# Attention and a mixture of experts on one core: newly searched orders for all five engines, and GpSimd steps that also wait for a named step

## What is computed

```python
x = x + attn(layernorm(x))      # causal; 3 query and key channels a head, 8 value channels a head
x = x + moe(layernorm(x))

# attn: scores[t,s] = scale * q3[t].k3[s] + (q3[t].dir) * (k3[s].dir); softmax over s <= t; out @ wo
# moe, for each of the 4096 tokens:
shared = gelu(xf @ Wfc_s + bfc_s) @ Wproj_s + bproj_s                 # 128 -> 512 -> 128
topk_p, topk_i = top_k(softmax(xf @ Wr), 2)                           # 8 experts, the best two
routed = sum over the two of gate * (gelu(xf @ Wfc[e] + bfc[e]) @ Wproj[e] + bproj[e])
```

## Time and profile before

| | us |
|---|---|
| median of 3 timed runs | 649.78 (647.6 to 656.1) |
| span of the profiled execution, first to last instruction | 693.1 |

### The profile page before, as it was taken

One profiled execution on the slowest core, in us unless ns is written; L12 is line 12 of the kernel. 1 busy time (PEld: TensorE's weight loads), 2 busy tenths in 40 slices (PEclk: granted clock), 3 DMA queues, 4 the chain that ended last, 5 costly groups with the idle time before them and its releaser, 6 DMA issues.

```text
span 693.1 us, 15803 instructions
## 1 busy us (share of the span) xinstructions
PE 577.4 (83%) x5284; PEld 433.5 (63%) x5318; DVE 444.3 (64%) x1179; ACT 423.6 (61%) x711; POOL 324.1 (47%) x434
## 2 busy tenths in 40 slices
PE   2678898999899799898897899999897787478686
PEld 2455464665465466565485778787776575377686
DVE  7799977699995966789844534555431245264386
ACT  4355776375666686396594599989998153134231
POOL 6817256475854657486445011122513576431440
PEclk9899998999999999999999899999999799599899
DMA  6182630063733010011526476857767287277661
GB/s 168 32 296 87 193 122 5 27 183 92 204 122 95 13 29 20 16 32 50 208 63 205 146 223 200 256 177 240 240 204 232 82 259 232 72 210 268 195 194 52
DMA packets 62429, 99.48 MB, mean 144 GB/s; under 512 B 9020, under 2 KB 47840, under 8 KB 61920
## 3 DMA queue, kind: packets, MB, share of 16 engines
q1 hardware_dynamic: 58512, 90.62, 43.1%
q0 software_dynamic: 3840, 7.87, 3.6%
HBM read 83.37 MB, written 31.80 MB: 166 GB/s over the span
## 4 chain that ended last, share of the span: by engine, by line
PE 38%; DVE 25%; ACT 16%; issue 9%; another core or an unknown queue 6%; POOL 3%; DMA 2%; SPq 0%; POOLq 0%; DVEq 0%; ACTq 0%
DVE negmax L1063 11%; PE banks L1425 7%; PE banks L1504 6%; PE banks L1512 5%; ACT hblk L961 5%; PE banks L1335 4%; ACT probs L923 4%; PE banks L1384 4%; ACT L961 3%; PE banks L1487 2%; PE banks L1386 2%; DVE probs L1208 2%; ACT L923 2%; PE banks L1482 2%
## 5 line engine op out<-in xcount | busy, mean ns | idle before, releaser
L1063 DVE TENSOR_REDUCE negmax<-banks 128x2 f32<-128x1024 f32 (+3 forms) x192 | 192.2, 1038 | 40.1 <-PE banks L1386 32.1
L923 ACT ACTIVATE probs<-banks 128x1024 f32<-128x1024 f32 x160 | 156.0, 1025 | 31.8 <-PE banks L1406 19.8
L792 POOL TENSOR_SCALAR_AFFINE_SELECT probs<-probs 128x512 f32<-128x512 f32 x128 | 79.6, 640 | 183.4 <-ACT probs L923 182.7
L961 ACT ACTIVATE hblk<-banks,wcur 128x128 f32<-128x128 f32 x340 | 95.3, 376 | 99.2 <-PE banks L1504 53.5
L1504 PE MATMUL banks<-xblkT,wcur 128*128 128x128 f32 x680 | 99.7, 291 | 25.2 <-ACT hblk L961 10.9
L1384 PE MATMUL banks<-kpad,qst 128*128 128x384 bf16 (+3 forms) x478 | 107.2, 296 | 15.6 <-DVE negmax L1063 9.1
L1504 PEld LDWEIGHTS banks<-xblkT,wcur 128*128 128x128 f32 x680 | 88.8, 202 | 32.1 <-ACT hblk L961 13.4
L1512 PE MATMUL banks<-wcur,hblk 128*128 128x128 f32 x680 | 93.2, 281 | 10.6 <-ACT hblk L961 4.2
L1386 PE MATMUL banks<-future,identb 128*128 128x128 bf16 x512 | 96.4, 220 | 5.3 <-ACT probs L923 1.9
L1512 PEld LDWEIGHTS banks<-wcur,hblk 128*128 128x128 f32 x680 | 83.9, 194 | 17.0 <-issue 6.2
L830 POOL DMA_INDIRECT got<-ys,from_row x56 | 55.1, 984 | 68.3 <-issue 30.2
(11 more groups left out here) (157 smaller groups left out, 862.0 us busy)
## 6 DMA issues: line engine op xcount, KB each, us to landing
wcur<-wtab SPq DMA_DIRECT2D x85, 578.0 KB
xs<-in_L_attn_x SPq DMA_DIRECT2D x8, 1188.0 KB, 8.7
xblk<-xs SPq DMA_DIRECT2D x85, 64.0 KB
ys<-yblk SPq DMA_DIRECT2D x34, 128.0 KB
kpad<-kst SPq DMA_DIRECT2D x64, 64.0 KB, 3.0
xs<-in_L_attn_x SPq DMA_DIRECT2D x8, 505.0 KB
acc<-in_L_attn_x SPq DMA_DIRECT2D x8, 256.0 KB, 5.1
wtab<-in_L_ffn_Wfc SPq DMA_DIRECT2D x2, 1024.0 KB
```

What stands on the lines that cost most here:

```text
L792: pool.affine_select(out=v, in_=v, compare_op=ALU.is_ge, fill=0.0, base=0, pattern=[[0, R], [1, P]], channel_multiplier=-1).then_inc(maske ...
L923: nc.scalar.activation(probs[:, g % 2, heads[0]:heads[-1] + 1, at:at + P * sum(EUNITS[unit])], src, ACT.Exp).then_inc(exp_done, 1)
L961: ins = nc.scalar.activation(hblk[:, k % 3, q, :], one(PLACE["HB", g, s])[:, P * q:P * q + P], ACT.Gelu_apprx_tanh, bias=wcur[:, k % NW, 2 ...
L1063: dve.tensor_reduce(negmax[:, g, tiles - 1, heads[0]:heads[-1] + 1], unit_view(PLACE["M", b, n], tiles), AX.X, ALU.max, negate=True).then_ ...
```

## The change

No step is added to any list or taken from it: the five lists hold the same steps (781 TensorE, 393 ScalarE, 492 VectorE, 234 GpSimd, 228 SyncE) in another order. 689, 301, 437, 199 and 206 of the places hold another step than before. Three things can be read off the new lists.

- The ScalarE list changes between exponential and gelu 36 times, before 60 times. Of the 24 that are gone 22 lie between `GB.0.0` and `GB.1.0`, two around `LX.4.0`.
- TensorE steps that need a single bank were in banks 4 to 7 only; now 156 of them are in banks 0 to 3, 66 of these ahead of `XT.0.0`.
- GpSimd waits, ahead of 18 `SC` or `GA` steps, for one more semaphore (`PACE`).

```diff
+PACE = {
+    ('SC', 5, 1): ('MX', 7, 19),
+    ('GA', 1, 2): ('YB', 1, 5),
+    ('GA', 2, 3): ('HB', 1, 12),
+    ('SC', 7, 3): ('HB', 1, 13),
+    ('SC', 7, 1): ('HB', 1, 15),
+    ('SC', 7, 0): ('YB', 1, 16),
+    ('GA', 3, 2): ('HB', 2, 0),
+    ('GA', 4, 1): ('HB', 2, 1),
...
+    ('GA', 5, 2): ('SB', 2, 8),
+    ('GA', 6, 0): ('HB', 2, 11),
+    ('GA', 6, 1): ('SB', 2, 10),
+    ('GA', 6, 3): ('SB', 2, 11),
+}
...
+            def hold_apart(kind, b, i):
+
+                if (kind, b, i) in PACE:
+                    step, at, n = PACE[kind, b, i]
+                    if step == "HB":
+                        pool.wait_ge(hblk_ready, nth("HB", at, n))
...
+                    elif step == "SB":
+                        pool.wait_ge(sums_ready, nth("SB", at, n))
...
                 elif kind == "SC":
+                    hold_apart(kind, b, n)
                     send_rows(b, n)
                 elif kind == "GA":
+                    hold_apart(kind, b, n)
                     get_rows(b, n)
```

A stretch of the ScalarE list, before and after:

```diff
-    GB.0.28 EX.7.0 HE.6.0 EX.7.1 GB.0.29 GB.0.30 EX.7.4 GB.0.31 GB.0.32 EX.7.2 GB.0.33 X2.6.0 GB.0.34 EX.7.3
-    GB.0.35 LX.6.0 EX.7.5 EX.7.6 OE.7.0 GS.6.3 GB.0.36 GB.0.37 EX.7.7 GB.0.38 GB.0.39 EX.7.8 GB.0.40 GB.0.41
...
+    OE.6.2 GB.0.25 GB.0.26 GB.0.27 GB.0.28 EX.7.1 EX.7.0 EX.7.4 GB.0.29 HE.6.0 GB.0.30 GB.0.31 GB.0.32 GB.0.33
+    EX.7.2 GB.0.34 X2.6.0 EX.7.3 LX.6.0 EX.7.5 GB.0.36 GS.6.3 GB.0.35 GB.0.37 OE.7.0 EX.7.6 EX.7.9 EX.7.7 EX.7.8
```

More of the change, by code:

```diff
@@ L72 @@
[L72 to L76, removed]
@@ new lines @@
+    TP.1.1@7 E.1.11@4 M.2.6@0 Y.0.2@6 E.1.10@42 TP.1.2@7 RK.0.0@1 Y.0.3@6 TK.3.0@7 M.2.7@2 M.2.8@4 TM.2.0@6
+    TQ.3.0@0 PV.1.3@7 M.2.9@4 T1.4.0@6 TP.1.3@7 M.2.13@2 M.2.10@0 TO.1.0@7 E.2.0@24 PJ.1.0@7 TQ.3.1@1 E.2.2@4
+    TM.2.1@6 M.3.5@0 M.3.11@7 M.2.16@2 E.2.5@4 M.2.23@6 TK.3.1@7 M.2.12@0 E.2.1@24 QKV.4.0@7 M.2.14@0 M.2.18@4
+    T2.1.0@6 M.2.22@2 M.2.19@0 RL.1.0@6 H.1.2@5 H.1.3@7 QKV.4.1@6 M.2.20@2 H.1.1@4 M.2.15@0 H.1.0@7 E.2.3@42
+    PV.2.0@6 Y.1.0@7 E.2.4@20 Y.1.1@7 M.2.21@4 Y.1.2@7 TK.4.1@3 M.3.2@0 TM.2.2@6 M.3.1@4 TK.4.0@2 TP.2.0@6
@@ new lines @@
+    TK.5.1@5 T2.3.0@4 M.5.0@2 M.4.21@0 M.5.2@6 H.3.0@4 E.4.8@2 H.3.2@5 RL.3.0@1 TM.4.3@0 PV.4.1@3 H.3.3@2
+    H.3.1@5 E.4.10@60 M.5.10@2 Y.3.0@5 RK.3.0@4 Y.3.1@5 M.5.4@2 E.4.11@0 QKV.6.1@4 M.5.7@6 E.4.9@2 Y.3.2@5
+    E.4.7@6 Y.3.3@5 M.5.3@2 M.5.17@4 M.5.6@6 TP.4.1@5 M.5.12@0 PV.4.3@3 M.5.8@4 PV.4.2@2 TM.5.0@3 M.5.9@0
+    M.5.13@4 E.5.0@62 QKV.6.0@1 TP.4.2@0 E.5.1@42 TM.5.1@7 TP.4.3@6 M.5.15@2 M.5.16@0 TO.4.0@6 T1.7.0@7 M.5.18@4
+    E.5.5@2 PJ.4.0@6 E.5.2@0 M.5.23@5 E.5.4@62 M.5.14@0 M.5.22@2 TK.6.0@5 E.5.3@60 QKV.7.1@4 M.5.19@2 TQ.6.0@7
@@ new lines @@
+    E.6.6@40 M.7.18@6 Y.5.0@2 XT.0.8@3 Y.5.1@2 YB.0.12@3 E.6.9@64 E.6.11@0 YB.0.13@3 HB.0.14@7 HB.0.15@6
+    HB.0.17@3 XT.0.9@5 HB.0.16@4 M.7.19@0 YB.0.14@7 XT.0.10@5 YB.0.15@7 YB.0.16@6 E.6.10@40 Y.5.2@2 HB.0.18@7
+    YB.0.17@6 HB.0.19@3 XT.0.11@6 Y.5.3@2 M.7.22@0 HB.0.20@5 M.7.23@7 HB.0.21@4 YB.0.18@6 TP.6.1@7 YB.0.19@6
+    E.6.8@0 E.6.7@42 PV.6.3@7 HB.0.22@6 YB.0.20@1 XT.0.13@0 YB.0.21@1 M.7.0@2 HB.0.23@7 XT.0.12@1 M.7.20@4
+    M.7.3@2 YB.0.22@6 M.7.2@0 YB.0.23@6 M.7.7@2 HB.0.24@7 M.7.1@4 PV.6.2@6 HB.0.25@7 HB.0.27@6 TM.7.0@5
@@ new lines @@
+    YB.0.24@4 XT.0.14@7 M.7.21@0 TP.6.2@3 HB.0.26@7 YB.0.25@4 HB.0.28@5 E.7.0@20 TP.6.3@7 YB.0.26@6 XT.0.15@4
+    YB.0.27@6 E.7.2@4 M.7.17@7 TO.6.0@6 HB.0.29@3 M.7.8@0 YB.0.28@2 HB.0.30@5 M.7.10@0 HB.0.31@7 YB.0.29@2
+    PJ.6.0@6 XT.0.16@5 M.7.6@0 YB.0.30@7 HB.0.32@6 HB.0.33@5 YB.0.31@7 XT.0.17@6 E.7.1@20 M.7.9@4 HB.0.34@7
+    M.7.13@4 YB.0.32@6 M.7.16@0 T2.6.0@5 YB.0.33@6 XT.0.18@7 TM.7.1@4 RL.6.0@5 HB.0.35@7 E.7.3@40 HB.0.36@6
+    HB.0.37@3 H.6.3@2 YB.0.34@1 PV.7.0@0 YB.0.35@1 H.6.2@7 E.7.5@0 RK.6.0@6 YB.0.36@3 XT.0.19@2 YB.0.37@3
@@ new lines @@
+    HB.1.21@5 YB.1.19@3 YB.1.20@6 Y.7.0@4 HB.1.22@7 Y.7.1@4 XT.2.0@5 YB.1.21@6 HB.2.0@7 Y.7.2@4 YB.1.22@6
+    YB.2.0@7 HB.2.1@5 XT.2.1@3 Y.7.3@4 XT.2.2@6 YB.2.1@7 HB.2.2@5 CM.2.0@4 HB.2.3@7 YB.2.2@6 HB.2.4@5 YB.2.3@6
+    XT.2.3@7 CM.2.1@4 HB.2.5@5 YB.2.4@3 CM.2.2@4 YB.2.5@3 CM.2.3@4 CM.2.4@4 XT.2.4@5 HB.2.6@7 HB.2.7@6 YB.2.6@7
+    CM.2.5@4 XT.2.5@6 YB.2.7@7 HB.2.9@5 HB.2.8@3 CM.2.6@4 CM.2.7@4 YB.2.8@7 XT.2.6@5 HB.2.10@6 YB.2.9@7
+    HB.2.11@3 YB.2.10@6 CM.2.8@4 HB.2.12@7 XT.2.7@5 YB.2.11@6 CM.2.9@4 HB.2.13@7 HB.2.14@6 CM.2.10@4 YB.2.12@7
@@ new lines @@
+    KE.2.0 OE.0.1 EX.0.13 EX.0.12 EX.0.19 EX.0.11 EX.0.10 KE.2.1 QE.2.0 OE.0.2 EX.0.15 EX.0.16 EX.0.18 EX.0.17
+    EX.1.0 EX.1.1 EX.1.4 OE.0.3 EX.1.2 EX.1.3 HE.0.0 EX.1.6 EX.1.5 OE.1.0 EX.1.9 EX.1.14 EX.1.7 EX.1.8 VS.3.0
+    EX.1.11 VS.3.1 EX.1.10 QE.2.1 X2.0.0 EX.1.13 EX.1.12 OE.1.1 LX.0.0 GS.0.2 GS.0.0 GS.0.1 GS.0.3 OE.1.2
+    EX.1.15 EX.1.16 EX.1.19 EX.1.17 EX.1.18 KE.3.0 OE.1.3 QE.3.0 HE.1.0 EX.2.0 XE.4.0 EX.2.1 EX.2.4 QE.3.1
+    EX.2.9 KE.3.1 EX.2.2 EX.2.3 VS.4.0 X2.1.0 LX.1.0 GS.1.2 VS.4.1 GS.1.3 GS.1.1 GS.1.0 EX.2.5 EX.2.6 EX.2.8
@@ new lines @@
+    SC.0.3 VX.3.0 N2.2.0 MK.3.3 MK.3.1 MK.3.2 MK.3.0 N1.6.0 BS.2.0 MK.3.4 SC.1.3 MK.3.5 MK.3.7 MK.3.6 SC.1.2
+    MK.3.9 MK.3.8 MK.3.11 MK.3.10 SC.2.2 MK.3.14 SQ.5.0 SK.5.0 MK.3.12 MK.3.13 MK.3.15 MK.4.0 SC.1.0 MK.4.2
+    MK.4.1 MK.4.3 VX.4.0 SC.2.3 N2.3.0 MK.4.6 MK.4.7 MK.4.5 MK.4.4 SC.2.0 MK.4.8 SC.2.1 MK.4.10 BS.3.0 SC.3.0
+    MK.4.14 MK.4.15 MK.4.13 MK.4.12 SC.3.2 MK.4.11 MK.4.9 N1.7.0 SK.6.0 MK.5.0 VX.5.0 SQ.6.0 N2.4.0 MK.5.3
+    MK.5.2 SC.3.3 MK.5.4 MK.5.1 SC.3.1 BS.4.0 MK.5.6 MK.5.7 MK.5.5 SC.4.1 SK.7.0 SC.4.0 SQ.7.0 SC.4.2 MK.5.8
@@ L280 @@
 AT = counted()
+PACE = {
[7 more added lines that the diff above has]
+    ('GA', 4, 1): ('HB', 2, 1),
+    ('GA', 4, 0): ('HB', 2, 2),
+    ('GA', 4, 2): ('HB', 2, 4),
+    ('GA', 4, 3): ('HB', 2, 5),
+    ('GA', 5, 0): ('YE', 2, 2),
+    ('GA', 5, 1): ('HB', 2, 7),
+    ('GA', 5, 3): ('YB', 2, 7),
+    ('GA', 5, 2): ('SB', 2, 8),
[3 more added lines that the diff above has]
+}
 def nth(kind, b, n=0):
@@ L818, in send_rows @@
                         in_=x2n[:, b % NX2, i, :], in_offset=None).then_inc(rows_sent[b % NX2], 16)
+            def hold_apart(kind, b, i):
[3 more added lines that the diff above has]
+                        pool.wait_ge(hblk_ready, nth("HB", at, n))
+                    elif step == "YB":
+                        pool.wait_ge(yblk_done, nth("YB", at, n))
+                    elif step == "YE":
+                        pool.wait_ge(yblk_ready, nth("YE", at, n))
+                    elif step == "MX":
+                        pool.wait_ge(m_taken, nth("MX", at, n))
+                    elif step == "SB":
+                        pool.wait_ge(sums_ready, nth("SB", at, n))
             def get_rows(b, i):
```

282 lines of the change are left out of this document (122 added, 160 removed).

## The result

| | before | after |
|---|---|---|
| timed runs, median of 4 each | 650.38 us (647.6 to 656.1) | 626.37 us (621.18 to 627.03) |
| ratio after to before, 95% interval | | 0.9636 (0.9573 to 0.9699) |
| recorded execution: span, its own time | 693.1 us, not given | 624.5 us, 626.19 us |

The change made the kernel 24 us faster. (The 649.78 us ahead of the prediction is the median of three of the four timed runs.)

A forecast was written before the change was run, and what follows sets the result against it. No engine fills the span, so stages bound the kernel; the middle stretch passes through gelu, block products and table loads. From 649.8 us, 12 for loads and 4 for the end give 634 us, range 612 to 654.

The forecast's parts named there:

- Table loads, 12 us: Middle stretch, 348 to 545 us: 22 ScalarE loads gone, 28.2 us, worth 12 us of time; ends 0 and 17.4.
- the halt: Piece without a releaser at 373 us in the middle stretch of the recorded execution, 8.7 us.
- its refutation: Forecast wrong if first block step to last `PV`, less the halt, stays at 188 us with ScalarE idle.
- TensorE is the bound already: Rival, middle stretch: table loads are hidden, worth 0 to 3 us; 643 to 650 us in all; chance 0.28.
- The price of a change of set: ScalarE: skill's 2.66 us would make 22 changes worth 58.5 us; the sum took the trace's 1.283 us load, no drain.
- The end, 4 us: Last gate matrices: `CB.6` moved behind them hides its fetch; between 0 and 6.1 us, taken as 4.
- Attention, 0 +- 5: Attention stage, up to 348 us: new banks and order gain 0, with 5 us either way.
- The rival of shared banks: Moved single-bank steps in banks 0 to 3 make TensorE wait for copies: slower, 664 us; chance 0.11.
- The 18 waits, 0: GpSimd's extra waits cost 0, 5 us loss at worst; span loses four halts, 37.4 us; timed runs gain 0.
- the halts are in the timed runs too: Rival: pacing GpSimd's DMAs takes half to all of 24.7 us more off timed runs, 609 to 622 us; chance 0.13.
- The sum for the span: Recorded execution: 693.1 - 37.4 - 12 - 4 = 639.7 us; 640 to 650 if short halts stay.
- Signs named for the profile: Profile after: among others, `XT.2.0` not waiting for rows, gate matrices back to back at the end without a fetch in the chain.

The follow-up runs named there:

- experiment 3: Kernel before with relu in place of gelu in the shared expert and blocks, so all table loads but one go: 644.5 us, 0.9935.
- experiment 7: Kernel before with `CB.6.0` and `CB.6.1` moved behind the last gate matrix (the run cited here): 647.25 us, 0.9989.
- experiment 1: Kernel after without the 18 extra waits, all five new lists kept: 627.23 us, 0.9654 to before.

## Why the prediction was right, and where its steps were not

The total and the direction were right; two terms of its sum, 12 and 4 us, were each wrong, one too large and one too small, and in part made up for one another. That the forecast came so near is in part luck.

- **Table loads, 12 us: the step that failed.** The count was right (687 ScalarE instructions for 711, 23 loads left in the middle stage, ScalarE busy 389.8 us for the forecast 393). Their worth was not: 59 loads fewer are 4.2 us in the old order, in the new one 35 of the 36 that remain are worth nothing that can be measured, and the whole new order up to `PV.7.2`, with the 22 loads gone in it, gives 7.5 us. The prediction bounded the gain by TensorE's idle time, 17.4 us, or 8.7 without the halt, and then took 12, above the second bound, though its sum was for runs without halts. In an undisturbed execution that idle time is 10.8 us before and still 9.4 after. The sign that it had named as its refutation came: 189.3 us from `XT.0.0` to `PV.7.2` in the shown execution, less the halt of 8.7, is 180.6, and after it is 181.6, with ScalarE waiting. The rival "TensorE is the bound already" was right about this stage, though not about the whole. The chain passed 29.7 us through loads, which was no measure here: a chain follows the one wait that ended last, and TensorE, busy 94% of the stage, was as near to ending it.
- **The price of a change of set.** The Trainium skill, "ScalarE: Activation LUTs", section "What ACT_TABLE_LOAD costs", puts a change of set at some 2.66 us, by which the 59 loads of experiment 3 would be an estimated 157 us of ScalarE. The trace has 1283 ns a load after as before and no drain beside it, and the run shows what the 59 are worth beside a busy TensorE: 4.2 us.
- **The end, 4 us: mis-sized, and by another mechanism.** It measured 11.7 us. The fetch of `CB.6` held the gate matrices in the trace, but its move alone gave nothing. Fetches did hold VectorE, in nine places; the waits at `CB.4` make the copies, stores and next fetches late. The prediction had counted that three combinations of fetched rows go behind `YE.1.11`, and gave it no price of its own. That this link carries the rest is read from the trace, not tried alone.
- **Attention, 0 +- 5: right**, 1.0007 for its order alone. The rival of shared banks is gone with it: TensorE's idle time in the attention stage is 51.5 us before and 46.6 after, and its waits for the row maxima at the line of the `M` scores fell from 9.0 us in 15 to

```profile
PE banks L1415 <- DVE negmax L1094: 4.8, 11, 1.2
```

- **The 18 waits, 0: right.** The cause given for the span, that the pacing does away with the halts, was wrong: they are absent without it, and absent from the kernel before in another execution. The rival "the halts are in the timed runs too" falls by that. The sum for the span, 639.7 us, came out 15 us too long (624.5): less its four long halts the shown execution was still 5 us longer than the second one, and the gain in span was 26 us, not 16.
- **Signs named for the profile.** No fetch held up `XT.2.0` (0.17 us), and the gate matrices stand back to back at the end, 2.05 us apart (`SB.2.11` to `SB.2.13` at 610.8, 612.9, 614.9); before, `SB.2.13` came 4.8 us behind `SB.2.12`.

**What stays open.** The new order up to `PV.7.2` gives 7.5 us (4.2 to 11.0). All loads of the old order are worth 4 us there; how much of the 7.5 the 22 missing ones are in the new order isn't known. The rest may be attention left for the time when blocks fill TensorE: in two recorded executions that have a matmul record for each of their 5318 weight loads (the move of `CB.6` in experiment 7, and experiment 1) 2926 and 2898 of its records lie ahead of `XT.0.0`, so 28 pass to the later stages. That wasn't tried apart. And 7.5 + 11.7 = 19.2 us of 23.7; the intervals, some 3 us each, can hold the rest, or the two parts help one another. The two results on loads also belong together: few loads win little in an order that hides them, yet the new order loses 21 us if 22 come back, so it seems to use the room that their absence leaves, unless the places where they were put back are to blame.

## What to carry to other kernels

Before a busy engine's work is costed as time, look at the stage in which it lies: where another engine is busy 95% there, what is removed can turn into waiting, as most of 28 us of table loads did here. In a written-out order look for a step that waits for a slow transfer ahead of a step that others need; but test by moving the whole tail, since the moves of one place that were tried gave nothing, and a store moved ahead of its data cost 6 us. And record a kernel twice before a stall without a releaser goes into a sum.

## What was not expected of the hardware

- Two recorded executions of one kernel differed by 42.5 us (693.1 and 650.6), nearly all of it in the five stalls put down to another core or an unknown queue, 39.5 us; no other recorded execution of these kernels had one.
- After 3.24 and 1.23 us of idle time with one product between, TensorE took 2.07 us for eight matmuls that take 1.06 elsewhere, that is 1.2 in place of 2.4 GHz. The window around it, before:

```profile
590.00:595.00 5.00, 1.76 (x16) 1.57 (x15) 2.12 (x10) 1.14 (x4) 0.00 (x0) 1.00 0.44 141
595.00:600.00 5.00, 3.77 (x22) 3.58 (x22) 0.65 (x3) 1.14 (x4) 0.00 (x0) 0.66 0.77 232
600.00:605.00 5.00, 5.00 (x47) 5.00 (x46) 3.18 (x7) 2.28 (x8) 0.00 (x0) 1.00 0.77 234
```

  So this stall of VectorE is paid twice: in the wait, and in the granted clock, 0.66 over the five microseconds from 595 us. Behind `YB.1.22` the clock is 0.94 before and 0.98 after.
- Seven recorded executions of the order of before, without halts, reach `XT.0.0` at 336 to 342 us; a single profile can't tell a few microseconds there.
